# Loading attention weight quarters ahead of modulation weights, with the orders of the vector, scalar and tensor engines to match

## What is computed

```python
mod = (silu(c) @ wmod).reshape(4, 6, 1, 1024)
sa, ca, ga, sb, cb, gb = (mod[:, i] for i in range(6))
ga = (2 * (ga >= 0) - 1) * maximum(abs(ga), 0.25)   # gb likewise
h = layernorm(x) * (1 + ca) + sa
x = x + ga * (h @ (weight * block_mask).T)          # block_mask: 32x32 blocks whose mask sum is > 0
h = layernorm(x) * (1 + cb) + sb
x = x + gb * ffn(h)                                 # silu(h@w1) * (h@w2) @ w3, weights decoded from 4-bit codes
```

## Time and profile before

| | us |
|---|---|
| median of 3 runs | 1575.6 (1574.91 to 1575.89) |
| the profiled execution, its own time | 1575.16 |
| span of the profiled execution | 1573.4 |
| PE busy | 1541.3 (98%) |
| DVE busy | 1033.3 (66%) |
| ACT busy | 986.9 (63%) |
| POOL busy | 5.5 |

### The profile page before, as it was taken

The page is one execution under the profiler, slowest core; times in us unless marked ns, Lnnn a source line. Parts: engine busy times, 40 slices in busy tenths (PEclk is TensorE's granted clock), DMA queues, the critical chain, the costliest instruction groups (busy, mean ns, idle before and its releaser), DMA issues.

```text
span 1573.4 us, 19155 instructions
## 1 busy us (share of the span) xinstructions
PE 1541.3 (98%) x7200; PEld 1271.2 (81%) x7200; DVE 1033.3 (66%) x1494; ACT 986.9 (63%) x1282; POOL 5.5 (0%) x10
## 2 busy tenths in 40 slices
PE   5889999999999999999999999999999999999999
PEld 3678888888888888888888888888888888888887
DVE  5787786554655455547676666666875758856994
ACT  3465676998888888883898988886333433333220
POOL 0000000000000000000000000000000000000000
PEclk9999999999999999999999999999999999999999
DMA  9965422465545455443778787786787968947973
GB/s 368 370 242 191 173 93 107 170 201 193 194 138 195 160 174 181 149 142 101 252 233 240 207 253 207 210 247 184 251 301 262 339 199 297 345 161 269 398 277 123
DMA packets 170139, 345.97 MB, mean 220 GB/s; under 512 B 14752, under 2 KB 65344, under 8 KB 170048
## 3 DMA queue, kind: packets, MB, share of 16 engines
q1 hardware_dynamic: 170048, 344.76, 64.9%
HBM read 249.77 MB, written 94.93 MB: 219 GB/s over the span
## 4 chain that ended last, share of the span: by engine, by line
PE 93%; DVE 3%; DMA 2%; ACT 1%; issue 1%; SPq 0%; ACTq 0%; DVEq 0%
PE ps L1895 10%; PE ps L1894 10%; PE ps L1893 10%; PE ps L1967 9%; PE ps L1966 9%; PE ps L1968 9%; PE ps L1904 9%; PE ps L1906 9%; PE ps L1905 9%; PE ps L1811 3%; PE ps L1813 3%; PE ps L1812 3%; DMA wmod<-wmod 2%; PE ps L1768 2%; PE ps L1751 1%; ACT modulated L887 1%
## 5 line engine op out<-in xcount | busy, mean ns | idle before, releaser
L842 ACT ACTIVATE w_raw<-w_raw 128x1024 f32<-128x1024 f32 x287 | 304.7, 1062 | 9.1
L1893 PE MATMUL ps<-ffn_in_hi,w_hi 128*128 128x512 f32 x688 | 268.6, 390 | 0.0
L1895 PE MATMUL ps<-ffn_in_hi,w_lo 128*128 128x512 f32 x688 | 267.8, 389 | 0.0
L1894 PE MATMUL ps<-ffn_in_lo,w_hi 128*128 128x512 f32 x688 | 267.7, 389 | 0.0
L1966 PE MATMUL ps<-t_hi,s_hi 128*128 128x512 f32 x616 | 239.6, 389 | 0.0
L1967 PE MATMUL ps<-t_lo,s_hi 128*128 128x512 f32 x616 | 239.6, 389 | 0.0
L1968 PE MATMUL ps<-t_hi,s_lo 128*128 128x512 f32 x616 | 239.6, 389 | 0.0
L1904 PE MATMUL ps<-x_m_hi,stream_hi 128*128 128x512 f32 x604 | 235.0, 389 | 0.0
L1905 PE MATMUL ps<-x_m_lo,stream_hi 128*128 128x512 f32 x604 | 235.0, 389 | 0.0
L1906 PE MATMUL ps<-x_m_hi,stream_lo 128*128 128x512 f32 x604 | 235.0, 389 | 0.0
L1088 ACT ACTIVATE s_hi<-s_raw 128x1408 fp32r<-128x1408 f32 x56 | 77.4, 1383 | 239.4 <-DVE s_raw L1603 191.2
(11 more groups left out here) (137 smaller groups left out, 2082.2 us busy)
## 6 DMA issues: line engine op xcount, KB each, us to landing
s_raw<-h_d SPq DMA_DIRECT2D x96, 704.0 KB, 5.6
stream_raw<-t_d SPq DMA_DIRECT2D x150, 256.0 KB, 3.4
t_d<-combined SPq DMA_DIRECT2D x106, 256.0 KB, 2.6
wmod<-wmod SPq DMA_DIRECT2D x12, 2048.0 KB, 15.4
t_raw<-w_d SPq DMA_DIRECT2D x88, 256.0 KB, 6.1
w_codes<-w12q SPq DMA_DIRECT2D x41, 512.0 KB, 5.3
h_d<-h_tile SPq DMA_DIRECT2D x44, 256.0 KB, 2.4
h_d<-up_c SPq DMA_DIRECT2D x44, 256.0 KB, 3.3
```

Of the source, the lines that this page charges most:

```text
L842: act.activation(RAWF[r], RAWF[r] if j else RQ[r][:], ACT.Prelu, bias=bias, scale=sign, alpha=slope).then_inc(line_ready, 1)
L1893: pe.matmul(acc, RH[r][:, k, :], HH[:, b, k, :], start=(k == 0), stop=False)
L1894: pe.matmul(acc, RH[r][:, k, :], HL[:, b, k, :], start=False, stop=False)
L1895: last = pe.matmul(acc, RL[r][:, k, :], HH[:, b, k, :], start=False, stop=(k == C - 1))
```

## The change

It reorders calls in four lists. No instruction is added, removed or resized.

- SP: quarter 0 of the weight is loaded ahead of `wmod` parts 0 and 1; quarters 1 and 3 ahead of parts 2 and 3.
- ACT: `weight_high(0)` goes ahead of `copy_rows(0)`; `weight_high(1)` and `weight_high(3)` go ahead of `copy_rows(1)`.
- DVE: `split_weight(0)` goes ahead of `read_mod(0)`; `split_weight(1)` and `split_weight(3)` go ahead of `read_mod(1)`, and so ahead of both `half_low_part1(1, .)`.
- PE: `attend_first(0, 1, 0)` goes between `modulation(2)` and `modulation(3)`; `attend_first(1, 1, 0)` goes ahead of `turn_mod(1, 1)`.

```diff
@@ SP
             load_mask(1)
+            load_weight(0)
             load_wmod(0)
             load_wmod(1)
-            load_weight(0)
             load_mask(2)
             load_mask(3)
             load_weight(2)
+            load_weight(1)
+            load_weight(3)
             load_wmod(2)
             load_wmod(3)
-            load_weight(1)
-            load_weight(3)
             sp.wait_ge(mask_step, MASK_STEPS + 2)
@@ ACT
                 start1(t)
+            weight_high(0)
             copy_rows(0)
-            weight_high(0)
             act.wait_ge(mod_read, 2)
             half_input1(0, 0)
             half_input1(0, 1)
             weight_high(2)
+            weight_high(1)
+            weight_high(3)
             copy_rows(1)
-            weight_high(1)
             act.wait_ge(mod_read, 4)
             half_input1(1, 0)
-            weight_high(3)
             half_input1(1, 1)
@@ DVE
             mask_weight(0)
+            split_weight(0)
             read_mod(0)
-            split_weight(0)
             half_low_part1(0, 0)
             sum_mask(2)
             half_low_part1(0, 1)
@@ DVE
             mask_weight(1)
+            split_weight(1)
+            split_weight(3)
             read_mod(1)
-            split_weight(1)
             half_low_part1(1, 0)
-            split_weight(3)
             half_low_part1(1, 1)
@@ PE
             modulation(2)
+            attend_first(0, 1, 0)
             modulation(3)
-            attend_first(0, 1, 0)
+            attend_first(1, 1, 0)
             turn_mod(1, 1)
-            attend_first(1, 1, 0)
             half_turn1(1, 1)
```

## The result

The changed kernel took 1587.17 us (median of 6 runs, 1586.66 to 1590.22), the kernel before 1575.74 us (6 runs, 1574.91 to 1577.18): +11.4 us. The ratio of the means is 1.0076 (95% interval 1.0063 to 1.0089). The profiled execution took 1587.58 us, its span is 1585.8 us, 12.4 more than before. The forecast was 1584.4, +8.8 against the median shown then (1575.6), the range 1577.5 to 1588.5.

A forecast was written before the change was run, and what follows sets the result against it. It took a start chained across engines as the bound. About half of +9.0 us was the first half's delay, the rest DVE and PE work ahead of read_mod(1): 1575.6 + 9.0 = 1584.6, given as 1584.4, range 1577.5 to 1588.5.

The forecast's parts named there:

- What bounds the kernel: A start of 117 us set by chains across engines, then PE never stops; only what moves the start counts.
- point E: End of half_low_part1(1, 0), 56.6 us before; forecast to move by +9.0, and the total with it.
- rival 2: PE's 4.5 us gap before norm1 absorbs the delay: 0 to +2 us, about 1576; chance 0.07.
- Transfers: Start: DMA is full, so quarters put ahead delay wmod part 1 by 2.7 us and part 3 by 5.6.
- the lower bound of +2.5: Smallest move of point E: s = +0.9, no loss to POOL, fast PE, chain running from part 3's landing.
- rival 1: Only the transfers count, the chain being part 3's landing plus fixed steps: +2.5 to +6, about 1579.5; chance 0.24.
- Rival 3: Quarters put ahead don't hold up wmod, as transfers share the engines: faster, about 1572; chance 0.04.
- s: Delay of the first half, through modulation(1) and WARM to block_mask(1): between +0.9 and +6.3, taken as +4.4.
- POOL against DVE: Second half: POOL's multiply of quarter 3 meets DVE's mask; loss 0, 1.75 or 3.65 us, taken as 1.75.
- the upper bound (3.65): Second half: the case that POOL's multiply comes first and DVE loses 3.65 us.
- PE's order and clock: Second half: attend_first(0, 1, 0) takes 4.4 us, modulation(3) 1.93 behind it; turn_mod(1, 1) starts at 61.4, ends 62.4.
- What follows is as before: Behind point E: nothing more is lost, and the 4.5 us gap moves along without shrinking.

The follow-up runs named there:

- e9: Kernel before, with ln1_sums(4) and set_aside(1) put ahead of low_part1(2) in DVE's list; 1573.7 us, ratio 0.9984.
- e7: Changed kernel with PE's order of before (both modulations first, turn_mod(1, 1) between the two products); 1584.58 us, ratio to before 1.0053.
- e10: Kernel before with the changed kernel's SP order, POOL's multiply held until mask_weight(1) is done, 6 useless matmuls between modulation(2) and modulation(3); 1579.26 us.
- e5: Changed kernel with a small memset in front of POOL's multiply, so that DVE's mask_weight(2) starts first; 1584.2 us, ratio to before 1.0049.
- e6: Changed kernel with POOL's multiply held back until mask_weight(1) is done; 1583.57 us, ratio to before 1.0047.
- e8: Changed kernel with 14 useless matmuls ahead of attend_first(0, 1, 0) and 8 ahead of half_turn1(1, 1) in PE's idle time; 1583.39 us.
- e2: Kernel before with only the change's second-half edits (SP from load_weight(1) on, ACT, DVE and PE); 1581.77 us, ratio 1.0038.

## Why the prediction was right, and where not

- *What bounds the kernel*: right. The start is a chain across engines, and what delays it goes through to the end (point E +10.3, the `norm1` wait's end +12.2, the span +12.4). That the 4.5 us gap doesn't absorb it (rival 2) is shown in the profile after, and by e9 from the other side.
- *Transfers*: right. `modulation(1)` starts at 24.96 (forecast 25.3), and the fourth part is there before its turn. Part 3 itself is seen in e7, where `modulation(3)` starts on it at 49.89 (forecast 50.19). The price by itself is 3.2 us (e10), close to the lower bound of +2.5, the core of rival 1. Rival 3, transfers out of order, didn't occur.
- *First half, s*: too high here. `modulation(1)` took 1.93, not the 3.64 that I took; s is +2.4, not +4.4. The two durations that I named both occur, 1.93 in seven profiles and 3.4 to 3.6 in three.
- *POOL against DVE*: too low. I argued from a gap of 0.11 us that DVE would be first and put in 1.75; POOL was first and it cost 3.47, about the upper bound (3.65). The mechanism was right in both directions (e5). What it costs on the path no run gives by itself, as e6's 3.6 has the clock and the hold in it. The Trainium skill (SBUF — State Buffer, section SBUF: two separate sides) calls it an exclusive lock held for a whole instruction; the rows of e5 agree, 5.67 and 3.67 us in place of 3.65 and 2.29.
- *PE's order and clock*: the order right (62.6 for `turn_mod`'s start, forecast 61.4), the clock too kind: 5.4 us for the 12 matmuls, not 4.4, and `modulation(3)` 2.3 instead of 1.9. I never asked what `copy_rows(1)` loses behind ACT's two roundings. In the changed kernel PE hid it, in e7 it is one of the two bounds.
- *"What follows is as before"*: the step that failed. PE has idle times around 64 to 67 us too, and its first products behind point E ran at the lower clock, 2.3 us more up to `turn1(2)`. I had named an idle time as a reason for the low clock in one place and not looked for it in the next. e8 shows the clock's two places together: 3.8 us.

The errors of s (-2.0) and POOL (+1.7) cancel, and that is luck. The clock's 1.0 and 0.4 us ahead of point E and the 2.3 us behind it make, with them, the 3.4 us between the forecast for the profiled execution (1584.2) and its time (1587.58). The median is 2.8 us above its forecast.

## What to carry to other kernels

When transfers fill the start, a load that is put ahead is paid for by every load behind it: ask which of them ends the chain, not which wait it removes. In lists written by hand, work that is ready early doesn't belong ahead of an item on which another engine waits; three repairs of one chain don't add up when other bounds lie right behind, and a repair can itself make one. The wait that is left after the start (here 4.5 us of PE, up to 117 us) is a place to look for gain: two pieces of DVE work moved into an existing wait gave 2.4 us, where the whole reordering of loads and lists lost 11.4.

## What the runs showed of the hardware

- When DVE and POOL wait for the same event, POOL was first in all six profiles with that constellation, by 0.01 to 0.02 us: for example 41.90 against 41.91 (changed kernel), 40.15 against 40.17 (e2). The loser's recorded duration holds its wait, 5.76 us instead of 2.29, and no idle time is shown in front of it.
- The same 32 matmuls of `modulation(1)`, after the same instructions, took 1.93 us in seven profiles and 3.4 to 3.6 in three. The level of PE's clock at a given place of the start isn't fixed by the program alone. One product of 12 matmuls took 2.9 us in e2, behind 1.5 us of idle time, and 5.4 us in the changed kernel, behind 3.7 us.
- The Trainium skill (TensorE: Matmul & The Clock Gate, section Part 1: The HAM clock gate) says that throttled is the default and that activity releases it; e8 agrees, where matmuls of no use brought 3.8 us.
